# A transformer block on eight cores: mean subtraction moved from Pool to VectorE, squares to ScalarE, last norm's sums ahead of a projection

## The chip, the cores and the metric

The kernel runs on one Trainium2 chip, on 8 cores, each with one of the eight sequences of the batch; the cores exchange nothing. The time is that of the slowest core, in microseconds (us). On a core, TensorE (PE in the rows) multiplies matrices, VectorE (DVE), ScalarE (ACT) and GpSimd (Pool) work element by element, and SyncE (SP) issues the DMAs.

## The reference

```python
def reference(x, Q_w, ..., O_w, O_b, U1, V1, b1, U2, V2, b2):   # x: (8, 2048, 1024) f32
    x = x + 0.5 * ffn(layernorm(x))
    x = x + attention(layernorm(x))      # 16 heads of 64, causal, softmax
    x = x + 0.5 * ffn(layernorm(x))
    return x
def ffn(x):                              # rank 256, 4096 hidden units
    return (gelu((x @ U1) @ V1 + b1) @ U2) @ V2 + b2
def layernorm(x):
    return (x - mean(x)) / sqrt(var(x) + 1e-5)
```

## The kernel before, in words

A core keeps its whole x (2048 tokens by 1024 features, f32) on chip, transposed: 8 tiles of 128 features on the partitions, the tokens in 4 chunks of 512 columns (`x[:, c, m, :]`). Its program has three parts.

The first FFN is `stream(F1, 4)`: 4 chunks of 32 steps. A step has two matmuls with V1 (`ffn_v1`, L253, L255), one GELU on ScalarE (L260), and two matmuls with U2 for the step two before (`ffn_u2`, L270). Everything else is hung into these steps by `put(chunk, step, function, ...)`, so each engine's queue gets it in that order. For chunk c that is, one chunk ahead, casts and squares of x (`ln1_prep`) and their sums over the features by matmuls with ones (`ln1_stat`), and at step 23 (29 in chunk 0) the reciprocal root and U1 (`f1_break`). For the chunk before, it is the eight output tiles (`ln2_tile`: two matmuls with V2 and, on VectorE, the addition to x, L295), the squares of each pair of tiles (`ln_square`), their sums (`ln2_stat`) and the scaling to bf16 (`ln2_scale`, L519). The half product of a chunk is evicted to `qm` at step 1 of the next (L279, L281). V2 and b2 are centred over the features at the end of chunk 0 (`center_v2`), so the FFN's output has mean zero once the mean of x is taken out of x (`x_center`, L484, one call a tile); what is taken out, with the mean of the FFN's output (`mean_out`), goes to DRAM and is added back to x in the second FFN (`mean_in`, L1449). So the second norm needs only the mean of squares.

Attention is a list of 320 steps, 40 for each of 8 head pairs (rounds). A step is two score matmuls (`qk_step`, L1033), one exponential on ScalarE (L1046), for the last blocks of a row a mask on Pool (L1055), and three steps later two matmuls with V (`av_step`, L1071). Between the steps, filler is drawn from a generator: in each round the projections of the next (`qk_proj`, `v_proj`), row maxima (`norm`, L735), and the bound that the exponential subtracts (`bound`, `bound_root`, `bound_out`). `share` says how many units of 216 ns of filler stand drawn after each step. A clock kept by the planner, `now`, advances by these estimates; `soon(ns, fn)` puts a piece of work off by that much of `now`, and `run_due` issues what is due. The two filler PSUM banks, 6 and 7, take turns (`main_bank`, `side_bank`).

Round 0 begins with the `bridge`: the last values of the first half, the output tiles of chunk 3 with its squares on ScalarE, its mean, the query and key projections of chunk 2, the sums, the root (`root`, L973 and L975) and the eight scalings of chunk 3, alternately on VectorE and Pool, two pairs of value projections with two row maxima among them, and the query and key projections of chunk 3, which read the scaled chunk 3. The zeros of the query buffer of round 1 are written by Pool as soon as the first FFN is over (`q_zeros(0)`, L890).

The second FFN is again a stream of 4 chunks. In it the mean is loaded at step 0 of a chunk and added at steps 20 to 27 on Pool; the next chunk's casts are on VectorE and its squares on Pool at steps 8 to 14; a chunk's outputs leave in the next chunk.

An engine works its queue in order. `Q.need(...)` is a wait on semaphores that Q's queue makes before its next instruction.

## Time and profile before

| | |
|---|---|
| median of 3 runs | 896.29 us |
| lowest and highest run | 896.21 and 990.42 us |
| profiled execution, whole | 894.62 us |
| its span, slowest core | 893.1 us (all cores 887.8 to 893.1) |
| TensorE busy | 825.9 us |
| VectorE, ScalarE, Pool busy | 418.8, 626.7, 280.2 us |
| mean granted TensorE clock | 0.985 of full |

One execution is profiled and the slowest core shown; starts count from the beginning of its span. The highest run stands far from the other two, which differ by 0.1 us. A wait in the rows is the idle time of an engine before an instruction, with the instruction that ended it.

### The profile page before, as it was taken

The page shows a single profiled execution, that of the slowest core. Times are in us where ns is not written, and L with a number is a line of the kernel's source. Part 1 is how long each engine was busy: PE and PEld are TensorE (multiplying, and loading weights), DVE is VectorE, ACT ScalarE, POOL GpSimd, SP SyncE. Part 2 cuts the span into 40 slices and gives each one's busy share as a digit, 9 for nine tenths or more (in the row PEclk, how much of TensorE's full clock was granted, in tenths as well). Part 3 has the DMA queues.
Part 4 walks back from the last instruction along what each step waited for, and adds up shares of the span by engine and source line. Part 5 has one row for each costly group of instructions (what it writes and reads, how often), then busy time and mean ns, then how long its engine had stood idle before and what let it go on. Part 6 is the DMA issues. An engine that isn't in the chain of part 4 may idle for free.

```text
span 893.1 us, 13052 instructions; the slowest of 8 cores (887.8 to 893.1 us)
## 1 busy us (share of the span) xinstructions
PE 825.9 (92%) x4122; PEld 398.3 (45%) x4122; DVE 418.8 (47%) x635; ACT 626.7 (70%) x791; POOL 280.2 (31%) x269
## 2 busy tenths in 40 slices
PE   4899889998699899999999999999789999999997
PEld 1344334543345445455454554544344444444442
DVE  2366666645556473643737436366243341233122
ACT  2665555557466688888888988899765636766764
POOL 0554975212423121312213122121232134071910
PEclk9899999999899999999999999999999999999999
DMA  9899001000012000300003000023600011022122
GB/s 261 257 334 313 18 25 48 1 1 1 1 58 97 1 1 1 107 24 25 1 1 107 25 25 1 1 78 112 212 0 1 1 31 18 31 77 84 24 94 95
DMA packets 17929, 57.83 MB, mean 65 GB/s; under 512 B 2116, under 2 KB 3524, under 8 KB 17352
## 3 DMA queue, kind: packets, MB, share of 16 engines
q1 hardware_dynamic: 17864, 57.00, 20.7%
q8 instruction: 36, 0.59, 0.3%
q14 instruction: 29, 0.24, 0.1%
HBM read 43.35 MB, written 13.64 MB: 64 GB/s over the span
## 4 chain that ended last, share of the span: by engine, by line
PE 77%; DVE 9%; issue 6%; ACT 5%; DMA 1%; POOL 1%; DVEq 0%; SPq 0%; ACTq 0%; POOLq 0%
PE ps L1033 12%; PE ps L270 12%; PE ps L1071 10%; PE ps L674 9%; PE ps L823 6%; PE ps L1228 6%; PE ps L253 6%; PE ps L255 6%; PE ps L194 3%; ACT pt L1046 2%; PE ps L226 2%; DVE QZ L697 2%; PE ps L731 2%; DVE yb L519 1%; PE ps L288 1%
## 5 line engine op out<-in xcount | busy, mean ns | idle before, releaser
L1046 ACT ACTIVATE pt<-ps,small 128x1024 bf16<-128x1024 f32 x320 | 321.2, 1026 | 98.6 <-PE ps L1033 91.7
L260 ACT ACTIVATE hb<-ps,cols 128x512 bf16<-128x512 f32 x256 | 173.5, 688 | 105.0 <-PE ps L255 104.2
L1055 POOL TENSOR_TENSOR pt<-pt,cb 128x256 bf16<-128x256 bf16 x128 | 85.8, 681 | 347.8 <-ACT pt L1046 300.7
L1033 PE MATMUL ps<-QZ,KM 128*128 128x512 bf16 (+1 forms) x640 | 177.6, 359 | 7.0 <-ACT pt L1046 5.8
L1071 PE MATMUL ps<-pt,V 128*128 128x512 bf16 (+3 forms) x640 | 170.8, 349 | 0.2 <-POOL pt L1055 0.2
L674 PE MATMUL ps<-yb,wqk 128*128 128x512 bf16 x512 | 139.8, 380 | 2.2 <-DVE small L735 1.1
L1071 PEld LDWEIGHTS ps<-pt,V 128*128 128x128 bf16 x640 | 62.6, 98 | 66.7 <-issue 2.9
L1033 PEld LDWEIGHTS ps<-QZ,KM 128*128 128x128 bf16 x640 | 60.6, 99 | 70.3 <-issue 25.6
L823 PE MATMUL ps<-wvb,yb 128*128 128x256 bf16 x512 | 74.1, 277 | 7.3 <-DVE small L735 6.6
L270 PE MATMUL ps<-hb,u2b 128*128 128x512 bf16 x256 | 78.1, 391 | 2.2 <-ACT hb L260 2.1
L270 PE MATMUL ps<-hb,u2c 128*128 128x512 bf16 x256 | 75.3, 379 | 1.8 <-ACT hb L260 1.4
L1096 DVE TENSOR_TENSOR attn<-ps,LR 64x512 bf16<-64x512 f32 x64 | 44.0, 688 | 59.0 <-ACT LR L1092 58.4
L674 PEld LDWEIGHTS ps<-yb,wqk 128*128 128x128 bf16 x512 | 48.5, 98 | 50.2 <-issue 5.7
L295 DVE SCALAR_TENSOR_TENSOR x<-ps,small,x 128x512 f32<-128x512 f32 x64 | 47.2, 749 | 44.5 <-PE ps L290 43.6
L697 DVE TENSOR_SCALAR QZ<-ps,cols 64x512 bf16<-64x512 f32 x64 | 47.9, 748 | 34.8 <-PE ps L674 27.1
L823 PEld LDWEIGHTS ps<-wvb,yb 128*128 128x128 bf16 x512 | 49.8, 99 | 31.2 <-issue 9.5
L1228 PE MATMUL ps<-attn,wo 128*128 128x512 bf16 x256 | 61.9, 379 | 1.4 <-DVE x L1238 0.8
L735 DVE TENSOR_REDUCE small<-ps 128x1 f32<-128x512 f32 x64 | 44.1, 689 | 28.3 <-PE ps L731 26.3
L253 PE MATMUL ps<-pb,v1b 128*128 128x512 bf16 x128 | 50.6, 395 | 3.3 <-DVE pb L236 3.3
L255 PE MATMUL ps<-pb,v1b 128*128 128x512 bf16 x128 | 50.3, 393 | 0.0
L484 POOL TENSOR_TENSOR x<-x,mu 128x512 f32<-128x512 f32 x32 | 45.8, 1461 | 12.6 <-DVE mu L450 12.6
L253 PE MATMUL ps<-pb,v1c 128*128 128x512 bf16 x128 | 48.5, 379 | 0.1
(133 smaller groups left out, 919.4 us busy)
## 6 DMA issues: line engine op xcount, KB each, us to landing
x<-x SPq DMA_DIRECT2D x16, 512.0 KB, 12.6
out<-x SPq DMA_DIRECT2D x32, 256.0 KB, 2.1
stg<-u SPq DMA_DIRECT2D x10, 512.0 KB, 11.5
stg<-v SPq DMA_DIRECT2D x10, 512.0 KB, 10.7
wos<-wo SPq DMA_DIRECT2D x8, 512.0 KB, 4.2
wst<-wq SPq DMA_DIRECT2D x7, 512.0 KB, 3.9
wst<-wk SPq DMA_DIRECT2D x7, 512.0 KB, 4.3
wst<-wv SPq DMA_DIRECT2D x6, 512.0 KB, 8.0
```

What stands on the lines that cost most here:

```text
L253: PE.run(lambda e: e.matmul(ps[:, b, :], F["v1"][:, fc // 4, 0, 128 * (fc % 4):128 * (fc % 4 + 1)], F["pb"][:, c % 2, 0, :], start=True, s ...
L255: t = PE.do(lambda e: e.matmul(ps[:, b, :], F["v1"][:, fc // 4, 1, 128 * (fc % 4):128 * (fc % 4 + 1)], F["pb"][:, c % 2, 1, :], start=Fals ...
L260: F["t_gelu"][g] = ACT.do(lambda e: e.activation(F["hb"][:, g % 4, :], ps[:, b, :], AF.Gelu_apprx_tanh, bias=cols[:, C_B1 + fc:C_B1 + fc + ...
L270: f = lambda e, m=m: e.matmul(ps[:, 3 + m, :], F["u2"][:, fc, 128 * m:128 * (m + 1)], F["hb"][:, g % 4, :], start=(fc == 0), stop=(fc == N ...
L674: f = lambda e, k=k: e.matmul(ps[:, b, :], wqk[:, which, k, :], yb[:, ch, k, :], start=(k == 0), stop=(k == NM - 1))
L697: toks.append(DVE.do(lambda e, r=r, h=h: e.tensor_scalar(QZ[s][r, h, csl], ps[r, b, :], cols[r, C_QB + p:C_QB + p + 1], None, OP.add)))
L823: f = lambda e, k=k, kt=kt, o=o: e.matmul(ps[:, b, o:o + 256], yb[:, kt // 4, k, 128 * (kt % 4):128 * (kt % 4 + 1)], wvb[:, k, :], start=( ...
L1033: f = lambda e, j=j, kt=kt: e.matmul(ps[:, 2 * sl + j, lo:TC], KM[s][:, 128 * kt:128 * (kt + 1)], QZ[s][:, h, TC * c + lo:TC * (c + 1)], s ...
L1046: t_e[i] = ACT.do(lambda e: e.activation(pt[:, i % 4, :, lo:TC], ps[:, 2 * sl:2 * sl + 2, lo:TC], AF.Exp, bias=bias, scale=0.125))
L1055: L["pt", i] = POOL.do(lambda e, v=v: e.tensor_tensor(v, v, mask, OP.mult))
L1071: f = lambda e, kt=kt, lo=lo, j=j: e.matmul(ps[:, b, lo:TC], V[gr % 2][:, kt, pr, 64 * h:64 * h + 128], pt[:, i % 4, j, lo:TC], start=(kt ...
L1228: f = lambda e, k=k: e.matmul(ps[:, b, :], wo[:, m, k, :], attn[:, c, k, :], start=(k == 0), stop=(k == NP - 1))
```

## The change

Seven things change. The subtraction of the mean (`x_center`) goes to VectorE and, for chunks 1 to 3, to steps 0, 1, 2, 5, 8, 11, 20 and 21 of the chunk itself, where it stood one chunk ahead. The squares of the second norm go to ScalarE for all chunks, at once after their tile for the first three. In the bridge the sums of chunk 3 come before the key projection of chunk 2, the root 400 ns of `now` after them, and all eight scalings are on VectorE, put off by 1500 + 700 m; filler issues them all before the query projection of chunk 3. The first score matmuls of round 0 wait for the zeros of their own buffer alone (`t_z[:2]`). The share of filler in round 0 begins at 13 units and grows by 4 for four steps, then by 6.5; in rounds 0 to 5 it ends one step later. The root of a round's bound is asked for 2700 after its last maximum, then each 1200, where it was 2300 and 900. In the second FFN the mean is added on VectorE at steps 22 to 29.

```diff
--- before.py
+++ after.py
@@ -480,8 +480,8 @@
 
     def x_center(c, m):
 
-        POOL.need(t_mu[c], L["c", c][m // 2])
-        F1["t_xin"][c, m] = POOL.do(lambda e: e.tensor_tensor(
+        DVE.need(t_mu[c], L["c", c][m // 2])
+        F1["t_xin"][c, m] = DVE.do(lambda e: e.tensor_tensor(
             x[:, c, m, :], x[:, c, m, :], mu[c], OP.subtract))
 
     def mean_out(c, b):
@@ -501,8 +501,7 @@
         t = ffn_v2(F1, c, m, b)
         if m % 2:
             def square():
-                q = ACT if c == NCH - 1 else POOL
-                L.setdefault(("s2", c), []).append(ln_square(q, m // 2, x[:, c], t, L["sqf"], sq))
+                L.setdefault(("s2", c), []).append(ln_square(ACT, m // 2, x[:, c], t, L["sqf"], sq))
             if c == NCH - 1:
                 soon(1500, square)
             else:
@@ -561,9 +560,8 @@
     put(0, 31, center_v2)
     for m in range(NM):
         put(0, 4 + 3 * m, x_center, 0, m)
-        put(1, 14 + m, x_center, 1, m)
-        put(1, 24 + m, x_center, 2, m)
-        put(2, 22 + m, x_center, 3, m)
+        for c in range(1, NCH):
+            put(c, (0, 1, 2, 5, 8, 11, 20, 21)[m], x_center, c, m)
     for c in range(1, NCH):
         for m in range(8):
             put(c, 3 + (3 * m) // 2, ln2_tile, c - 1, m, (7, 5, 6)[m % 3])
@@ -962,7 +960,6 @@
         yield 1
         yield 1
         yield from qk_proj(0, 0, 2)
-        yield from qk_proj(0, 1, 2, ACT)
         if len(L["s2", 3]) < 4:
             run_due(1e12)
         b = main_bank()
@@ -974,15 +971,18 @@
             ACT.need(tl)
             L["r2", 3] = ACT.do(lambda e: e.activation(rstd[:, 0, :], var[:, 0, :], AF.Exp, scale=-0.5))
             for m in range(NM):
-                ln2_scale(3, m, POOL if m % 2 else DVE, 0)
+                soon(1500 + 700 * m, lambda m=m: ln2_scale(3, m, DVE, 0))
 
         for m in range(NM):
             yield 1
-        root()
+        soon(400, root)
+        yield from qk_proj(0, 1, 2, ACT)
         yield from norm_mid(0, v_proj(0, 8), [(0, 2)])
         yield from norm_mid(0, v_proj(0, 10), [(1, 2)])
         bound0((2,))
         soon(1500, lambda: bound0_root((2,)))
+        while t_yb[3] is None:
+            run_due(agenda[0][0])
         yield from qk_proj(0, 0, 3)
         wqk_cast(1, 0)
         if ("u0", 2) not in L:
@@ -1023,7 +1023,7 @@
         lo = 256 if r == n - 1 else 0
         sl = i % 2
         if p == 0:
-            PE.need(t_z, t_QK[0, 0, c], [t_QK[0, 1, j] for j in range(c + 1)])
+            PE.need(t_z[:2], t_QK[0, 0, c], [t_QK[0, 1, j] for j in range(c + 1)])
         PE.need(t_e.get(i - 2), t_QK[p] if p else None)
         if i < 2:
             PE.need(bank_free[2 * sl], bank_free[2 * sl + 1])
@@ -1153,7 +1153,7 @@
             bank_at = now[0] + 1300
             if n == 7:
                 bound(p + 1)
-                root_at = now[0] + 2300
+                root_at = now[0] + 2700
 
         def small(n, u):
             nonlocal root_at
@@ -1161,7 +1161,7 @@
                 yield from one_norm(pend.pop(0))
             elif root_at is not None and ("u", p + 1) not in L and now[0] >= root_at:
                 bound_root(p + 1)
-                root_at += 900
+                root_at += 1200
             elif root_at is not None and ("u", p + 1) in L and now[0] >= max(root_at, bank_at) and u <= 5:
                 root_at = None
                 yield from bound_out(p + 1)
@@ -1384,10 +1384,10 @@
                 win = window(p) if p < NP - 1 else window7()
                 acc = 0
                 if p == 0:
-                    share = {k: 6.0 * (k + 1) for k in range(12)}
-                    share.update({k: 72 + v for k, v in spread(p, 12, 37, 24 + 96 + 9).items()})
+                    share = {k: 13 + 4 * k if k < 4 else 25 + 6.5 * (k - 3) for k in range(12)}
+                    share.update({k: 77 + v for k, v in spread(p, 12, 38, 19 + 96 + 9).items()})
                 elif p < NP - 2:
-                    share = spread(p, 0, 37, 96 + 9)
+                    share = spread(p, 0, 38, 96 + 9)
                 elif p == NP - 2:
                     share = spread(p, 0, 35, 64 + 9)
                 else:
@@ -1445,8 +1445,8 @@
         t_mu2[c] = ld_mu2[c % 2].load(SP, mu2[:, c % 2, :], s_mu[c:c + 1, :].partition_broadcast(128))
 
     def mean_in(c, m):
-        POOL.need(t_mu2[c], L["c3", c][m // 2], t_x2[c][m])
-        F2["t_xin"][c, m] = POOL.do(lambda e: e.tensor_tensor(
+        DVE.need(t_mu2[c], L["c3", c][m // 2], t_x2[c][m])
+        F2["t_xin"][c, m] = DVE.do(lambda e: e.tensor_tensor(
             x[:, c, m, :], x[:, c, m, :], mu2[:, c % 2, :], OP.add))
 
     def out_tile(c, m, b):
@@ -1479,7 +1479,7 @@
             put(c, 21, f2_break, c)
         put(c, 0, mean_load, c)
         for m in range(8):
-            put(c, 20 + m, mean_in, c, m)
+            put(c, 22 + m, mean_in, c, m)
     stream(F2, NCH)
     for m in range(NM):
         out_tile(3, m, (5, 6, 7)[m % 3])
```

## Rows read from the trace of the kernel before

**Rows 1.** Page, busy time, share and instructions of TensorE and its weight loads.

```profile
PE 825.9 (92%) x4122; PEld 398.3 (45%) x4122; DVE 418.8 (47%) x635; ACT 626.7 (70%) x791; POOL 280.2 (31%) x269
```

**Rows 2.** Table of stretches: length, busy time by engine, PEclk, DMA share, GB/s.

```profile
205.00:262.00 57.00, 44.36 (x238) 23.33 (x236) 28.57 (x45) 34.30 (x46) 20.98 (x19) 0.94 0.02 3
...
303.00:359.00 56.00, 54.02 (x302) 28.95 (x303) 28.98 (x49) 48.61 (x59) 11.22 (x16) 1.00 0.00 1
```

**Rows 3.** TensorE's waits, 60 to 125 us: total, times, longest.

```profile
PE ps L288 <- DVE qm L279: 4.7, 2, 2.9
PE ps L194 <- DVE yb L178: 2.7, 1, 2.7
```

**Rows 4.** TensorE's waits, 205 to 250 us.

```profile
PE ps L823 <- DVE small L735: 5.9, 1, 5.9
PE ps L731 <- ACT var L973: 1.6, 1, 1.6
PE ps L288 <- DVE x L295: 1.3, 2, 0.6
PE ps L1033 <- ACT pt L1046: 1.0, 1, 1.0
PE ps L674 <- DVE small L806: 0.9, 1, 0.9
PE ps L1033 <- POOL QZ L890: 0.7, 1, 0.7
```

**Rows 5.** Timeline, chunk 1: start, duration, instruction, idle time before it.

```profile
87.39 12.97 POOL L484 TENSOR_TENSOR x<-x,mu 128x512 f32<-128x512 f32 x8
...
91.25 1.75 DVE L178 CAST yb<-x 128x1024 bf16<-128x1024 f32 x1
...
108.78 10.39 DVE L519 TENSOR_TENSOR yb<-x,rstd 128x512 bf16<-128x512 f32 x8
```

**Rows 6.** Timeline, the end of chunk 0.

```profile
70.54 0.68 DVE L279 TENSOR_SCALAR qm<-ps 128x512 bf16<-128x512 f32 x1
...
71.47 0.38 PE L288 MATMUL ps<-qm,v2b 128*128 128x512 bf16 x1 [1.77 <-DVE qm L279]
```

**Rows 7.** Timeline, the last scalings and a row maximum.

```profile
231.70 5.70 DVE L519 TENSOR_TENSOR yb<-x,rstd 128x512 bf16<-128x512 f32 x4 [4.88 <-ACT rstd L975]
...
237.92 0.67 DVE L735 TENSOR_REDUCE small<-ps 128x1 f32<-128x512 f32 x1
```

**Rows 8.** Groups by line: min/median/max ns (or, last two, busy, mean, idle).

```profile
L484 POOL TENSOR_TENSOR x<-x,mu x32: 1262/1284/1777, 24.8 to 156.2; 128x512 f32<-128x512 f32 x32
...
L186 POOL TENSOR_TENSOR sq<-x x12: 1893/1894/2342, 74.9 to 181.6; 128x1024 bf16<-128x1024 f32 x12
...
L519 DVE TENSOR_TENSOR yb<-x,rstd x8: 681/686/693, 198.7 to 203.8; 128x512 bf16<-128x512 f32 x8
...
L185 ACT ACTIVATE sq<-x x4: 1042/1044/1047, 214.8 to 221.8; 128x1024 bf16<-128x1024 f32 x4
...
L260 ACT ACTIVATE hb<-ps,cols 128x512 bf16<-128x512 f32 x256 | 173.5, 688 | 105.0 <-PE ps L255 104.2
...
L295 DVE SCALAR_TENSOR_TENSOR x<-ps,small,x 128x512 f32<-128x512 f32 x64 | 47.2, 749 | 44.5 <-PE ps L290 43.6
```

**Rows 9.** Table of stretches around waits.

```profile
95.00:100.00 5.00, 3.51 (x11) 1.43 (x12) 2.91 (x3) 0.60 (x1) 5.00 (x4) 0.75 0.01 3
...
120.00:125.00 5.00, 4.97 (x24) 2.29 (x25) 1.82 (x3) 2.06 (x3) 1.52 (x1) 1.00 0.00 2
235.00:240.00 5.00, 1.26 (x7) 0.92 (x8) 4.19 (x5) 0.00 (x0) 4.15 (x4) 0.74 0.00 0
240.00:245.00 5.00, 5.00 (x21) 2.81 (x20) 1.76 (x5) 1.56 (x4) 0.67 (x1) 0.57 0.00 0
```

**Rows 10.** Timeline, the end of chunk 2.

```profile
167.91 0.38 PE L288 MATMUL ps<-qm,v2b 128*128 128x512 bf16 x1 [0.19 <-ACT qm L281]
```

**Rows 11.** TensorE's waits, 360 to 600 us.

```profile
PE ps L761 <- ACT small L755: 2.2, 4, 0.5
```

## The prediction

> **What bounds the kernel now.** I read the shares of the page first [rows 1]: TensorE is busy 825.9 us, 92% of the span. So only its idle time, some 67 us, and time at a lower clock can be won, and the table of stretches says where it lies. The attention rounds lose little: 303 to 359 is 56.00 us with 54.02 busy, clock 1.00. The stretch 205 to 262, in which the last FFN tiles of chunk 3, its second norm and the first attention steps share the engines, is 57.00 us with 44.36 busy and clock 0.94 [rows 2]: 12.6 us idle and 0.06 x 57 = 3.4 us of clock. Then the table of TensorE's waits of each such stretch: who ended them. Between 60 and 125 us it names two [rows 3]; between 205 and 250 five that matter [rows 4]. Last the timeline around the longest, to see what the releasing engine had been doing [rows 5, 6, 7].
>
> **Work leaves Pool.** The mean's subtraction costs Pool 1.28 us (median) each, 32 times, and the squares 1.89 each, 12 times [rows 8]. Neither is on TensorE's path itself; the harm is what VectorE does meanwhile. Eight scalings ran at 10.39 / 8 = 1.30 us apart beside a busy Pool, and a cast took 1.75 [rows 5]; the same scaling takes 0.686 with Pool idle [rows 8], some 0.62 apart in a row of them. That the neighbour is the cause is a reading: nothing else differs so plainly. The Trainium skill's page SBUF — State Buffer, section "SBUF: two separate sides", says that a VectorE instruction with two SBUF inputs and a Pool instruction that reads SBUF lock each other out for a whole instruction. By that rule the scalings fall to the lone pace once Pool is quiet; if instead the slow pace had another cause it would stay, and chunk 1 would keep its waits (the third rival). The trace agrees with the rule, 1.30 against 0.62.
>
> **Chunk 1 of the first FFN, the sums of the next chunk.** TensorE waits 2.7 us for a cast [rows 3], and in 95 to 100 the clock is 0.75 [rows 9]: 0.25 x 5 = 1.3 us. Pool had eight subtractions in a row from 87.39 to 100.4 [rows 5]. After the change none stands there. Four casts, four squares and two smaller evictions, ten pieces of about 0.69 each, are 6.9 us; TensorE's own work up to there (four steps of 0.86, the mean's matmuls, the eight of the sums) is some 7. Saved: 2.7 + 1.3 = 4.0 us; bounds 2.7 and 4.7.
>
> **Chunk 1, its end.** The eviction of the half product waits behind the eight slow scalings; of all such waits (4.7 us, two [rows 3]) this one is 2.9. Scalings at 0.62 end near 108.78 + 5.0 = 113.8, before the eviction can start at about 116.3. Two subtractions of chunk 2 now stand ahead of it, 1.24 us, ready earlier too. The same place one chunk later, with Pool's scalings out of the way, waits 0.19 [rows 10]. Saved 2.7; bounds 1.5 and 2.9.
>
> **Chunk 0, its end.** Here the eviction stands behind the centring of V2 and starts at 70.54, and TensorE waits 1.77 us for it [rows 6]. The subtractions of chunk 1 are now queued at steps 0 and 1, ahead of it: 2 x 0.62 = 1.2 us later, all of it on the path. The wait of 3.0 us could cost clock as well: after a wait of 2.9 us the next slice showed 1.00, after 5.9 us 0.57 [rows 9, 4]. So 1.2, bounds 0 and 3.0.
>
> **Squares on ScalarE.** The trace has four of them, 1.044 us each [rows 8]. Twelve more stand between the GELUs, four a chunk, one in three steps with two output tiles. Three steps are, for TensorE, 3 x 4 + 4 matmuls at 0.216 us (1.73 us for each of the eights) = 3.46 us; for ScalarE 3 x 0.69 + 1.05 = 3.12. It fits, barely. Each square also waits for VectorE's eviction, some 0.5 us after its GELU, so the next GELU comes about 1 us late, and TensorE runs its second product two steps behind: it feels 0 to 0.1 us. I take 0.5 us in all; bounds 0 and 6 (0.5 for each of 12). Subtractions at steps 5, 8 and 11 lie between pairs of tiles and cost VectorE only slack.
>
> **First attention steps.** The first score matmul waits 0.7 us for Pool to write zeros that another buffer needs [rows 4]; the narrower wait removes that. More filler ahead of the first steps (13 units, then 4 a step, against 6 a step) puts an output tile where TensorE waits 1.0 for an exponential, and spreads the rest, where it waits 1.3 for evictions [rows 4]. Stepping through the order with two matmuls of 0.216 a tile and an eviction of 0.75 [rows 8], the last tile ends near 215.5 with one step pair (0.86) less done, against 218.7: 2.4 us saved; bounds 0.7 and 3.
>
> **The last sums and scalings.** This is the largest term. From 231.70 four scalings on VectorE take 5.70 us, 1.42 each, with the other four on Pool beside them, and a row maximum of 0.67 us stands behind them; TensorE waits 5.9 for it, after 1.6 for the bank which the root's first half holds [rows 7, 4]. In 235 to 245 the clock is 0.74 and 0.57, with 1.26 and 5.00 busy [rows 9]: 0.26 x 1.3 + 0.43 x 5 = 2.5 us of clock (up to 3.4 by the whole stretch). Then 0.9 for the copy of the exponent's shift [rows 4]. Together 1.6 + 5.9 + 2.5 + 0.9 = 10.9 us. After the change the sums come before the key projection of chunk 2, whose 1.73 us then cover the root, and the scalings are queued 0.7 us apart, so a maximum has at most one or two before it. What becomes late next: the squares of chunk 3 on ScalarE, as the sums come some 5 us sooner (0.7 us), and the eight scalings, 5.0 us, with about 4.5 us of maxima and evictions between them must be done before the query projection of chunk 3. 18 units of filler and three steps, some 6.3 us of TensorE's work, lie between; 9.5 less 6.3 and less the 1.8 by which the first scaling can start ahead of that work leave a wait of 1.4 us. The shift's 0.9 stays. 10.9 - 0.7 - 1.4 - 0.9 = 7.9, saved; bounds 4 and 10.
>
> **Attention rounds.** The root of each round's bound is asked for 0.4 us later and the filler ends one step later. TensorE waits for that root 2.2 us in four rounds [rows 11]; some of it may go, or return where the filler runs out. I take 0.8 saved, bounds 3 saved and 2 lost. Second FFN: the mean is added by VectorE, 0.69 against Pool's 1.26, in steps 22 to 29, when VectorE has nothing to do and no output waits; 0. Cover gone (it would have to pass the next eviction): 0.7.
>
> **The sum.** 4.0 + 2.7 - 1.2 - 0.5 + 2.4 + 7.9 + 0.8 = 16.1 us. The profiled execution took 894.6 us (span 893.1 and 1.5 around it), so 878.5; the median of the runs shown is 896.3, 1.7 more. I put the time at 880.2 against that median, -1.8%. Two per cent, about what a measurement of this kernel can tell from no change, is 17.9 us: the boundary is 878.4.
>
> **Rivals.**
> First: *the scalings are cleared wholly* (the window 225 to 250 falls to the pace of the later rounds, no new wait). For it: a later round loses 2 us in 56 [rows 2]. Then 10 instead of 7.9, 3 instead of 2.4, 2 instead of 0.8 in the rounds, and nothing for the squares: 4.0 + 2.7 - 1.2 + 3 + 10 + 2 = 20.5, so 875.8 against the median. Chance 0.33.
> Second: *the stall moves inside the bridge*. All scalings now lie on one engine, which also evicts values and takes maxima; if they bunch because the root is late, a maximum again has several before it, TensorE idles some 3 to 4 us and the clock falls once more. For it: TensorE's whole 5.9 us wait came from one maximum behind queued scalings. Against it: 0.62 each instead of 1.42. Then 7.9 becomes 2, the total 10.2: 886.1. Chance 0.14.
> Third: *VectorE's slow pace is not Pool's doing*. Then casts and scalings stay slow, chunk 1 keeps its 4.0 and 2.7, and the added operations bunch the bridge by 3: 894.6 - 16.1 + 6.7 + 3 = 888.2, 889.9 against the median. Chance 0.04.
> Fourth, slower than before: *the squares hold up the GELUs*. A square waits for an eviction with the GELUs behind it. TensorE's page (TensorE: Matmul & The Clock Gate, "Architectural detail: the array is 16× 32×32") says that ScalarE's queue is strictly in order, so nothing passes a waiting square. As a mechanism of this kernel: if GELUs have less lead than I count, each of the 12 squares costs TensorE 0.5 of waiting and 1.05 of work, 18.6 us, more than the 16.1 + 0.5 won: 894.6 + 2.0 + 1.7 = 898.3. It decides from 16.6 / 12 = 1.4 us a square. Against it: ScalarE is idle 105.0 us over 256 GELUs [rows 8], 0.41 a step, and 1.73 us of extra matmuls go with each two squares. Chance 0.03.
>
> **How the numbers follow.** The forecast 0.46, the rivals 0.33, 0.14, 0.04, 0.03. The likeliest is 880.2. The forecast's own terms range from about 875 to 885. The range 872.5 to 888.0 takes in the first and second rival and leaves out the last two and the extremes of the first. Faster by over 2% is the first rival (0.33, of which a little falls short) and a part of the forecast's lower side, 0.38 in all; within 2% 0.60; slower by over 2% 0.02, as the fourth alone would have to cost twice its price.
>
> **What would show it.** Scalings and casts at about 0.69 in chunk 1, no wait of the sums near 93 us and no slice below 1.00 there; a wait near 3 us at the end of chunk 0; squares of 1.05 between GELUs without TensorE waiting for them; the first score matmul not waiting for Pool; no wait above 2 us and no slice at half clock between 215 and 250. I am wrong if VectorE stays at 1.3 us with Pool idle, or if a new wait above 3 us stands before the query projection of chunk 3.

## The result and the profile after

The changed kernel takes 874.73 us (median of 4 runs: 874.05, 874.41, 875.05 and one of 896.72), the kernel before 896.21 and 896.29 beside it: ratio 0.9757, of the medians without the 896.72, with a 95% interval of [0.9729, 0.9786]. Executions in which one die ran at a lower clock for long stand in no comparison, here and below. On another chip a kernel whose instruction lists are the changed kernel's on every engine (a2 below) took 874.83 against 894.57, ratio 0.9782 [0.9766, 0.9797]; this one has the narrower footing and is used below. So the change wins 19.5 us, -2.2%. The forecast was 880.2 in a range of 872.5 to 888.0: the time is in the range and 5.5 us below the forecast, nearest to the first rival's 875.8.

The page, busy time by engine, to be read against [rows 1]:

```profile
PE 819.7 (94%) x4122; PEld 397.2 (45%) x4122; DVE 448.3 (51%) x703; ACT 638.0 (73%) x803; POOL 166.1 (19%) x189
```

Pool lost 114 us of work and VectorE gained 29.5, ScalarE 11.3. TensorE's busy time fell by 6.2 us with the same 4122 matmuls, which speaks of the clock. Its idle time fell from 893.1 - 825.9 = 67.2 to 873.5 - 819.7 = 53.8.

Where the 19.6 us between the two spans (893.1 and 873.5) were won is read from landmarks: matmuls and evictions that both kernels have once. First the kernel before, then the changed one, in the timeline: the first and the last small matmul of the bridge, the one at the end of round 0, the one ahead of the last round, and the last half product.

```profile
209.53 0.58 PE L800 MATMUL ps<-small,cfs 128*128 128x2 f32 x4 [0.50 <-DVE V L836]
262.17 0.58 PE L800 MATMUL ps<-small,cfs 128*128 128x1 f32 x4 [0.64 <-ACT small L793]
303.83 0.58 PE L761 MATMUL ps<-small,cfs 128*128 128x1 f32 x4 [2.81 <-ACT small L755]
632.65 0.58 PE L761 MATMUL ps<-small,cfs 128*128 128x1 f32 x4 [2.42 <-ACT small L755]
882.34 0.69 DVE L279 TENSOR_SCALAR qm<-ps 128x512 bf16<-128x512 f32 x1 [17.97 <-PE ps L270]
```

```profile
203.59 0.58 PE L798 MATMUL ps<-small,cfs 128*128 128x2 f32 x4 [0.50 <-DVE V L834]
246.64 0.50 PE L798 MATMUL ps<-small,cfs 128*128 128x1 f32 x4
287.22 0.58 PE L759 MATMUL ps<-small,cfs 128*128 128x1 f32 x4 [0.95 <-DVE V L834]
612.10 0.99 PE L759 MATMUL ps<-small,cfs 128*128 128x1 f32 x4 [2.43 <-ACT small L753]
862.79 0.69 DVE L279 TENSOR_SCALAR qm<-ps 128x512 bf16<-128x512 f32 x1 [13.16 <-PE ps L270]
```

The lead of the changed kernel is 5.9 us at the first pair, 15.5 at the second, 16.6, 20.6 and 19.6 at the others. So the first FFN gave 5.9, the bridge 9.6, the rest of round 0 1.1, rounds 1 to 6 together 3.9, and the last round with the second FFN took 1.0 back.

The slowest core is another one in each kernel (4 before, 7 after), and not all of the 5.9 is the change's. ScalarE evicts its part of the half product of chunk 0 at 69.09 before and at 67.57 after; over the eight cores that time spreads from 63.8 to 69.1 before and from 64.4 to 67.6 after, and as widely in kernels whose instructions up to there are the same. So 1.5 of the 5.9 is where these two cores happened to stand. The medians over the eight cores of each profiled execution, in us:

| stretch | before | after |
|---|---|---|
| start to that eviction in chunk 0 | 66.8 | 66.2 |
| to the first small matmul of the bridge | 142.2 | 136.0 |
| to the last of the bridge | 52.7 | 43.0 |
| to the one at the end of round 0 | 41.7 | 40.6 |
| rounds 1 to 6 | 328.8 | 324.7 |
| last round, to the first half product of the second FFN | 141.3 | 142.2 |
| to the last half product | 108.4 | 108.4 |
| to the end | 9.9 | 10.9 |

"By landmarks" below means these stretches.

**First FFN.** TensorE's waits between 60 and 125 us, of the changed kernel, against [rows 3]:

```profile
PE ps L288 <- DVE qm L279: 3.0, 1, 3.0
```

The cast and the second `qm` are gone, and one wait of 3.0 us stands where 1.8 stood. Its timeline at the end of chunk 0, and below it the stretches around it and around the chunk 1 sums:

```profile
69.03 1.29 DVE L484 TENSOR_TENSOR x<-x,mu 128x512 f32<-128x512 f32 x2
70.23 0.69 DVE L279 TENSOR_SCALAR qm<-ps 128x512 bf16<-128x512 f32 x1
71.17 0.38 PE L288 MATMUL ps<-qm,v2b 128*128 128x512 bf16 x1 [2.99 <-DVE qm L279]
73.22 0.63 PE L253 MATMUL ps<-pb,v1b 128*128 128x512 bf16 x1
```

```profile
70.00:75.00 5.00, 3.83 (x11) 1.45 (x12) 2.27 (x4) 0.62 (x1) 0.00 (x0) 0.67 1.05 360
95.00:100.00 5.00, 5.00 (x25) 2.25 (x23) 2.95 (x4) 2.10 (x4) 1.94 (x2) 1.00 0.39 133
```

The two subtractions stand ahead of the eviction, as the forecast said, and TensorE waits 1.2 us more. After the wait a matmul takes 0.63 instead of 0.38 and the clock of the slice is 0.67: another 0.33 x 5 = 1.65 us. On one of the eight cores, core 3, the same wait cost no clock (last section). At the sums of chunk 1 (95 to 100) the 0.75 of [rows 9] has become 1.00.

**Bridge.** The stretch that [rows 2] shows with 44.36 busy at 0.94:

```profile
205.00:262.00 57.00, 51.36 (x282) 26.71 (x281) 36.97 (x64) 40.76 (x51) 14.63 (x17) 1.00 0.14 41
```

TensorE's waits, 195 to 250 us, against [rows 4]:

```profile
PE ps L1071 <- POOL V L882: 1.8, 1, 1.8
PE ps L729 <- DVE V L834: 1.4, 1, 1.4
...
PE ps L672 <- DVE yb L518: 0.7, 1, 0.7
```

The waits for the maximum (5.9), for the root's bank (1.6), for an exponential (1.0) and for Pool's zeros (0.7) are gone. Two are new: 1.8 for Pool's writing of ones into V (it begins at 242.58, behind a mask, and takes 1.81; before, at 258.4, nobody waited for it), and 1.4 for an eviction of values that stands behind paced scalings. What the paced scalings look like, in the timeline of VectorE and TensorE:

```profile
221.29 0.69 DVE L733 TENSOR_REDUCE small<-ps 128x1 f32<-128x512 f32 x1
221.90 0.68 DVE L518 TENSOR_TENSOR yb<-x,rstd 128x512 bf16<-128x512 f32 x1
...
227.04 0.59 PE L672 MATMUL ps<-yb,wqk 128*128 128x512 bf16 x2 [0.67 <-DVE yb L518]
```

A maximum goes through between scalings, and the query projection of chunk 3 waits 0.67 us.

### The profile page after: what moved, and what is told of

It is laid out like the page before. It is cut to its first block, busy times and chain, and to the rows that moved or that the text cites. A ratio compares the mean times of both kernels' runs of the same rounds, so it can differ in the third digit from the quotient of the medians.

```text
span 873.5 us, 13011 instructions; the slowest of 8 cores (870.0 to 873.5 us)
## 1 busy us (share of the span) xinstructions
PE 819.7 (94%) x4122; PEld 397.2 (45%) x4122; DVE 448.3 (51%) x703; ACT 638.0 (73%) x803; POOL 166.1 (19%) x189
## 4 chain that ended last, share of the span: by engine, by line
PE 79%; ACT 6%; DVE 6%; issue 5%; DMA 2%; POOL 0%; DVEq 0%; SPq 0%; ACTq 0%; POOLq 0%
PE ps L1033 12%; PE ps L672 12%; PE ps L270 11%; PE ps L1071 11%; PE ps L1228 6%; PE ps L253 6%; PE ps L255 6%; PE ps L821 4%; PE ps L194 4%; ACT pt L1046 3%; PE ps L226 2%; PE ps L288 1%; PE ps L290 1%; DMA stg<-v 1%; PE ps L729 1%
## 5 line engine op out<-in xcount | busy, mean ns | idle before, releaser
L1033 PEld LDWEIGHTS ps<-QZ,KM 128*128 128x128 bf16 x640 | 60.7, 99 | 67.6 <-issue 22.5
L270 PE MATMUL ps<-hb,u2b 128*128 128x512 bf16 x256 | 76.2, 383 | 2.6 <-ACT hb L260 2.1
L253 PE MATMUL ps<-pb,v1c 128*128 128x512 bf16 x128 | 48.5, 379 | 0.1
L255 PE MATMUL ps<-pb,v1c 128*128 128x512 bf16 x128 | 48.5, 379 | 0.0
```

The lines of the kernel that those rows point to most:

```text
L253: PE.run(lambda e: e.matmul(ps[:, b, :], F["v1"][:, fc // 4, 0, 128 * (fc % 4):128 * (fc % 4 + 1)], F["pb"][:, c % 2, 0, :], start=True, s ...
L255: t = PE.do(lambda e: e.matmul(ps[:, b, :], F["v1"][:, fc // 4, 1, 128 * (fc % 4):128 * (fc % 4 + 1)], F["pb"][:, c % 2, 1, :], start=Fals ...
L270: f = lambda e, m=m: e.matmul(ps[:, 3 + m, :], F["u2"][:, fc, 128 * m:128 * (m + 1)], F["hb"][:, g % 4, :], start=(fc == 0), stop=(fc == N ...
L1033: f = lambda e, j=j, kt=kt: e.matmul(ps[:, 2 * sl + j, lo:TC], KM[s][:, 128 * kt:128 * (kt + 1)], QZ[s][:, h, TC * c + lo:TC * (c + 1)], s ...
```

## The experiments

My theory, once the result was known: the gain has four sources (VectorE rid of Pool's company in the first FFN, the bridge's order, its pacing, and something in the rounds that I had priced too low), each to be found again by undoing it alone. The rival: the gain is the bridge's, and the rounds drift with whatever state the bridge leaves them in. All kernels are the changed one with the edit shown, except e1. The kernel before took 894.46, 894.57, 894.89 and 896.03 us on the four chips, so a part's worth is told from the ratio: (ratio - 0.9782) x 895. Each ratio is uncertain by some 1.5 us, a difference of two by some 2; where that is too coarse, the landmarks of all eight cores are set beside it.

**The rounds: a1, a2, a3.** Both round edits undone, then each alone:

```diff
-                root_at = now[0] + 2700
+                root_at = now[0] + 2300              # a1, a2
-                root_at += 1200
+                root_at += 900                       # a1, a2
-                    share = spread(p, 0, 38, 96 + 9)
+                    share = spread(p, 0, 37, 96 + 9)   # a1, a3
```

> The changed kernel with the root of each round's bound asked for at 2300 and 900 again, and the filler of rounds 1 to 5 ending at step 37 again. The changed kernel's rounds 1 to 6 are 3.9 us shorter than before (54.9 against 55.5 us a round). If these two edits did that, this kernel takes 874.7 + 3.9 = 878.6 us and its rounds are 55.5 us long. If the forecast's 0.8 us was right and the rounds are shorter for another reason (what they inherit from round 0), it takes about 875.5 us and its rounds stay at 54.9.

> The changed kernel with only the times of the bound's root as before (2300 and 900). Undoing both edits of the rounds cost 3.7 us (878.4). Theory: the later root gives it, since asked for early it sits in ScalarE's queue ahead of the exponential and TensorE waits 0.5 us for it, then for the exponential, at the narrow last step of a row: 877 to 878.4, rounds of 55.3 to 55.5 us. Rival: the filler's one step more (37 to 38) gives it, and this kernel stays at 874.7 to 875.5 with rounds of 54.9.

> The changed kernel with only the filler of rounds 1 to 5 ending one step earlier again (37). Theory that the root gives the gain: 874.7 to 875.5. Rival: the filler's extra step gives it: 877 to 878.4 and rounds of 55.3 to 55.5 us, with TensorE idle at the end of a round.

Measured: a1 878.37, ratio 0.9817 [0.9802, 0.9832]; a2 874.83, 0.9782 [0.9766, 0.9797]; a3 875.41, 0.9781 [0.9766, 0.9797]. Together the edits are worth 3.1 us, each alone nothing by the ratio: a2's instruction lists are even those of the changed kernel, so the later root alone moves nothing once the filler ends a step later. By landmarks rounds 1 to 6 take 328.5 us in a1, 324.7 in a2 and 326.0 in a3, so a3 has lost 1.2 of the 3.8 there, and its total hides it (its last round is 0.6 shorter). One round, from one root to the next, in a1 and then in the changed kernel (table of stretches):

```profile
386.84:442.27 55.43, 54.29 (x300) 28.59 (x301) 28.77 (x48) 49.53 (x59) 12.61 (x19) 1.00 0.03 11
```

```profile
392.07:447.08 55.01, 54.03 (x300) 28.61 (x301) 29.84 (x48) 49.70 (x59) 12.42 (x18) 1.00 0.00 1
```

0.42 us in this round; the three others between such roots differ by 0.9 each (a1 222.3 us for the four, the changed kernel 219.2), 3.1 in all. Where it comes from, in the timeline of a1 around the bound's root (L751 and L753; the small matmuls behind it are L759):

```profile
441.82 0.20 ACT L753 ACTIVATE small<-small 128x1 f32<-128x1 f32 x1
441.93 0.67 ACT L1046 ACTIVATE pt<-ps,small 128x512 bf16<-128x512 f32 x1
442.27 0.58 PE L759 MATMUL ps<-small,cfs 128*128 128x1 f32 x4 [0.55 <-ACT small L753]
...
443.40 2.20 ACT L1046 ACTIVATE pt<-ps,small 128x1024 bf16<-128x1024 f32 x2 [0.80 <-PE ps L1033]
```

and of a2, the same place:

```profile
446.15 0.20 ACT L753 ACTIVATE small<-small 128x1 f32<-128x1 f32 x1
446.38 1.12 ACT L1046 ACTIVATE pt<-ps,small 128x1024 bf16<-128x1024 f32 x1
446.61 0.58 PE L759 MATMUL ps<-small,cfs 128*128 128x1 f32 x4 [0.35 <-ACT small L753]
...
448.17 1.12 ACT L1046 ACTIVATE pt<-ps,small 128x1024 bf16<-128x1024 f32 x1 [0.16 <-PE ps L1033]
```

In a1, as before, the root falls into the narrow last step of a row: its exponential has 512 columns and lasts 0.67, not 1.12. TensorE stands 0.55 us in front of the small matmuls, the next scores come late, and ScalarE, with so short an exponential to bridge it, idles 0.80. In a2 the root falls into a full step: 0.35, then 0.16. The waits from 330 to 600 us, TensorE's and then ScalarE's, of a1:

```profile
PE ps L759 <- ACT small L753: 3.0, 5, 0.8
```

```profile
ACT pt L1046 <- PE ps L1033: 24.0, 56, 0.8
```

and of the changed kernel:

```profile
PE ps L759 <- ACT small L753: 1.8, 5, 0.4
```

```profile
ACT pt L1046 <- PE ps L1033: 20.8, 60, 0.8
```

TensorE's own wait is 1.2 us longer in a1, ScalarE's for scores 3.2 us, which is the size of the whole loss.

The other rounds show the same: behind the root ScalarE's exponential lasts 0.67 five times in a1 and five times before, and 1.10 or 1.12 each time in a2, a3 and the changed kernel. Either edit takes the root out of the narrow step, which is why neither alone is missed much. The rival falls here: a1 has the bridge of the changed kernel (43.0), and its rounds have the pace of before (55.53 before, from 405.11 to 460.64).

**The mean and the squares in the first FFN: b1, b2, b3, b3r.** b1 gives the subtraction back to Pool at its old steps (which is not its old time, see below), b2 to Pool at the new steps, b3 and b3r the squares of chunks 0 to 2 back to Pool.

```diff
-        DVE.need(t_mu[c], L["c", c][m // 2])
-        F1["t_xin"][c, m] = DVE.do(lambda e: e.tensor_tensor(
+        POOL.need(t_mu[c], L["c", c][m // 2])                      # b1, b2
+        F1["t_xin"][c, m] = POOL.do(lambda e: e.tensor_tensor(     # b1, b2
-        for c in range(1, NCH):
-            put(c, (0, 1, 2, 5, 8, 11, 20, 21)[m], x_center, c, m)
+        put(1, 14 + m, x_center, 1, m)                             # b1
+        put(1, 24 + m, x_center, 2, m)                             # b1
+        put(2, 22 + m, x_center, 3, m)                             # b1
-                ... ln_square(ACT, m // 2, x[:, c], t, L["sqf"], sq)
+                ... ln_square(ACT if c == NCH - 1 else POOL, ...)  # b3, b3r
```

> The changed kernel with the subtraction of the mean on Pool again, at the steps of before. Theory: Pool beside VectorE slows the casts and scalings of chunk 1; the waits of 2.7 us for the cast and 2.9 us for the half product come back and the one at the end of chunk 0 falls from 3.0 to 1.8 with its clock loss: 4.0 + 2.7 - 1.2 to 2.8, so 4 to 5.5 us more, 879 to 880. Rival: the squares, now on ScalarE, were the harmful part of Pool's load, and with them gone Pool's subtractions cost nothing: 873 to 875.

> The changed kernel with the subtractions on Pool, but at the changed steps (chunks 1 to 3: 0, 1, 2, 5, 8, 11, 20, 21). It parts the engine from the place. If the harm of before is Pool's instructions beside VectorE's casts and scalings, the new place alone takes most of them away from these: 875 to 876.5, and the wait at the end of chunk 0 falls below 3.0 since VectorE no longer has the two subtractions ahead of the half product's eviction (unless these wait for Pool's lock on the centring of V2). If the engine matters wherever it stands: 879 to 880 as with both undone.

> The changed kernel with the squares of chunks 0 to 2 on Pool again. Theory: they cost TensorE nothing on ScalarE (0.5 us at most) and little on Pool, where only the casts of the next chunk meet them: within 1 us of 874.7, and VectorE's casts near them take 1.0 to 1.9 instead of 0.69. Rival: Pool's squares delay the sums of each chunk, 2 us or more.

> The changed kernel with the squares of chunks 0 to 2 on Pool again, once more. The one undisturbed look gave 877.3, with a wait of 1.0 us for the cast ahead of the sums in chunk 1. Theory: Pool's squares push into VectorE's casts there, as before: 876 to 877.5. Rival: the squares are worth nothing and the look was high: 874.5 to 875.5.

Measured: b1 879.52, 0.9829 [0.9812, 0.9845], so 4.2 us; b2 876.33, 0.9784 [0.9763, 0.9805]. b3 gave a single time to go by, 877.32 beside 894.46, and no ratio, so it was repeated as b3r: 876.22, 0.9784 [0.9767, 0.9801]. So of b1's 4.2 us most is the place. The engine alone and the squares lie within the error: 0.2 each by the ratio, though b2 stands 1.5 us above a2 on the same chip, and b3's time 2.4 above 0.9782 of the 894.46 beside it. By landmarks the first FFN takes 136.0 in the changed kernel, 139.8 in b1, 136.6 in b2, 137.2 in b3 and 136.8 in b3r: 3.8, 0.6, 1.2 and 0.8 more; the last three are small beside the 1.7 by which cores of one kernel differ there. TensorE's waits 60 to 125 us of b1, then of b3r (b2 has one wait for `qm`, 3.7):

```profile
PE ps L288 <- DVE qm L279: 7.1, 2, 3.7
```

```profile
PE ps L288 <- DVE qm L279: 3.0, 1, 3.0
PE ps L194 <- DVE yb L178: 1.2, 1, 1.2
```

b1 has two `qm` waits again but not the cast's, and the one at the end of chunk 0 is 3.7, not the 1.8 that I expected back; the squares alone bring back 1.2 of the cast's 2.7. Pool's timeline in b1 shows why:

```profile
59.23 10.29 POOL L484 TENSOR_TENSOR x<-x,mu 128x512 f32<-128x512 f32 x8 [0.74 <-DVE mu L450]
```

Pool works its queue in order. In the kernel before, the four squares of chunk 0 stood ahead of chunk 1's subtractions and held them back to 87.39 [rows 5], onto the casts. With the squares on ScalarE the same eight, at the same steps, start at 59.23, as soon as the mean is there, and fall onto the centring of V2; in b2 they do too, at 59.74. So b1 does not undo the subtraction as it was: the cast's 2.7 needed Pool's squares ahead of Pool's subtractions, and no run has these subtractions back at their old time with the squares on ScalarE. What b1 and b2 differ in is chunk 2's subtractions, eight in a row from 98.6 to 109.4 in b1, with Pool's casts of weights behind them. What it costs VectorE to have Pool beside it shows in b1's scalings of chunk 1:

```profile
105.38 10.92 DVE L518 TENSOR_TENSOR yb<-x,rstd 128x512 bf16<-128x512 f32 x8
```

They take 4.90 in the changed kernel. In b2 (and b1) the same is true of the centring of V2 ahead of `qm`: its cast L375 lasts 1.28 beside Pool's subtraction and 0.22 without, which makes 3.0 us of waiting 3.7.

**The bridge whole: b4.** Key projection ahead of the sums, root at once, scalings at once and alternately on Pool, the old share and the wait for all zeros:

```diff
+        yield from qk_proj(0, 1, 2, ACT)       # ahead of the sums
-        soon(400, root)
+        root()
-                soon(1500 + 700 * m, lambda m=m: ln2_scale(3, m, DVE, 0))
+                ln2_scale(3, m, POOL if m % 2 else DVE, 0)
-                    share = {k: 13 + 4 * k if k < 4 else 25 + 6.5 * (k - 3) for k in range(12)}
+                    share = {k: 6.0 * (k + 1) for k in range(12)}
-            PE.need(t_z[:2], ...)
+            PE.need(t_z, ...)
...  (and without the loop that issues all scalings ahead of the query projection)
```

> The changed kernel with the bridge as before: sums after the key projection, root at once, scalings alternating between VectorE and Pool and all at once, the old share of round 0, the wait for all zeros. Theory: the bridge is worth 9.8 to 10.5 us by itself, so 884.5 to 885.2, with the wait of some 6 us and slices at half clock back. Rival: the first FFN's part hands the bridge a better start, and the bridge alone is worth 6 or less: 881 or less.

Measured: 885.17, 0.9897 [0.9881, 0.9914], so the bridge is worth 10.3 us (by landmarks 8.8 in it and 1.1 in the rest of round 0). Its waits are those of before, and so is the clock behind them (waits 195 to 250 us, and a stretch):

```profile
PE ps L821 <- DVE small L733: 5.9, 1, 5.9
PE ps L729 <- ACT var L971: 1.6, 1, 1.6
```

```profile
235.00:240.00 5.00, 5.00 (x23) 2.82 (x21) 1.76 (x5) 1.72 (x4) 0.67 (x1) 0.65 0.00 0
```

**Inside the bridge: c1, c2, c3, and e1 on the kernel before.** c1 keeps the pacing but has the scalings alternately on VectorE and Pool. c2 has all on VectorE but asks for them at once. c3 puts the key projection ahead of the sums again and keeps the rest. e1 is the kernel before with that one order changed.

```diff
-                soon(1500 + 700 * m, lambda m=m: ln2_scale(3, m, DVE, 0))
+                soon(1500 + 700 * m, lambda m=m: ln2_scale(3, m, POOL if m % 2 else DVE, 0))   # c1
+                ln2_scale(3, m, DVE, 0)        # c2
```

```diff
-        yield from qk_proj(0, 1, 2, ACT)       # e1: ahead of the sums, in the kernel before
...
         root()
+        yield from qk_proj(0, 1, 2, ACT)       # e1: behind the root; c3 is the reverse
```

> The changed kernel with the last eight scalings again alternately on VectorE and Pool, but still paced 700 apart. The bridge is worth 10.4 us in all. Theory: Pool's share makes VectorE's scalings slow (1.4 instead of 0.7 us) and Pool's own take 1.7, so the chunk is ready later and the maxima wait: 2 to 4 us more, 877 to 879. Rival: pacing alone takes care of it, as two engines share the work: 874 to 875.5.

> The changed kernel with all eight scalings on VectorE but queued at once after the root. Theory: a maximum or an eviction stands behind up to eight scalings of 0.62 us, 5 us; the sums' early place leaves some 2 us of cover, so a wait of 2 to 3 us and perhaps clock: 876.5 to 879. Rival: they start earlier than paced ones and are cleared before the first maximum is due, so the time is 873.5 to 875.

> The changed kernel with the key projection of chunk 2 again ahead of the sums, so only the order undone; scalings stay on VectorE and paced. Theory: without these 1.7 us of cover TensorE waits for the bank that the root holds (1.6 us as before) and for the scaled chunk (1 to 2 us more): 877 to 878.5. Rival: engine and pacing alone give the gain, 874.7 to 875.5.

> The kernel before with one edit: the key projection of chunk 2 after the sums and the root. Scalings still alternate, unpaced. If the order carries the bridge, its 1.7 us of filler and a step hide the 1.6 us wait for the bank and part of the 5.9 us wait, and with them the half clock: 5 to 8 us less than before, 887 to 890. If the maximum behind four slow scalings (5.7 us) still stops TensorE, it gains 1.5 to 3 us: 892 to 893.

Measured: c1 874.38, 0.977 [0.9755, 0.9785]; c2 877.89, 0.9805 [0.9788, 0.9821]; c3 883.84, 0.9867 [0.9846, 0.9889]; e1 891.9, 0.996 [0.9945, 0.9976]. So the engine of the scalings is worth nothing that can be told (-1.1; by landmarks c1's bridge is 0.5 longer and its rounds 0.6 shorter), which misses my theory of 2 to 4. The pacing is worth 2.1: the intervals overlap in part, but c2's bridge is 2.2 to 2.4 longer on every core. The order is worth 7.6 taken out last (6.1 to 8.2 by landmarks) and 0.004 x 895 = 3.6 put in first. Waits 195 to 250 us of c2, then of c3, then of e1 (200 to 255, lines of before):

```profile
PE ps L821 <- DVE small L733: 3.0, 1, 3.0
```

```profile
PE ps L672 <- DVE yb L518: 4.7, 1, 4.7
PE ps L729 <- ACT var L971: 2.4, 1, 2.4
```

```profile
PE ps L823 <- DVE small L735: 3.5, 1, 3.5
```

c2 has the second rival's mechanism: a maximum stands behind eight scalings in a row (5.38 us in its timeline), yet it costs 3.0 us, since they take 0.67 each. c3 shows what the order hides: with the sums late, paced scalings are too late for the query projection. Pacing pays only with the sums early; e1 shows that early sums take 2.4 of the 5.9 us off even with all scalings at once and half of them on Pool.

**Mean in the second FFN back on Pool: a4.**

```diff
-        DVE.need(t_mu2[c], L["c3", c][m // 2], t_x2[c][m])
-        F2["t_xin"][c, m] = DVE.do(lambda e: e.tensor_tensor(
+        POOL.need(t_mu2[c], L["c3", c][m // 2], t_x2[c][m])
+        F2["t_xin"][c, m] = POOL.do(lambda e: e.tensor_tensor(
-            put(c, 22 + m, mean_in, c, m)
+            put(c, 20 + m, mean_in, c, m)
```

> The changed kernel with the mean added back on Pool again, at steps 20 to 27 of the second FFN. The forecast's term is 0: nothing waits for it and VectorE has no fast SBUF work beside it; 874.7 within 0.5. Rival: Pool's additions slow something of the second FFN, 1 us or more.

Measured: 873.56, 0.976 [0.9743, 0.9778]. That is 2.0 us less than the changed kernel, with intervals that just touch; its times (873.05 to 873.80) lie below all eight of a2 and a3 on the same chip (874.60 to 876.98). TensorE's waits from 640 to 880 us are the same four lines in both, and from 720 to 800 its busy time is 78.87 in both. So VectorE for this addition brings nothing, and the landmarks say what it costs: from the last half product to the end a4 takes 9.7 to 10.3 us on its eight cores, the kernel before 9.7 to 10.8 and the changed kernel 10.6 to 11.9; medians 9.8, 9.9 and 10.9. The last computing instruction ends 7.1 us after that eviction in all of them; why the outputs then end later is not shown. What else a4 is ahead by is not the edit's: up to the second FFN its instructions are the changed kernel's, and four of its cores, against one of the changed kernel's, happened to lose no clock at the end of chunk 0.

**Repairs of what the change left: d1, d2, d4.** d1 lets the values' product wait for the ones of its own buffer only. d2 centres the first half of V2 two steps earlier and apart from the second. d4 has both, and the first two subtractions behind the eviction of `qm`.

```diff
-        PE.need(L["pt", i], [...], t_one)
+        PE.need(L["pt", i], [...], t_one[gr % 2])       # d1, d4
-    put(0, 31, center_v2)
+    put(0, 29, center_v2, (0,))                         # d2, d4, ahead of f1_break
+    put(0, 31, center_v2, (1,))
-            put(c, (0, 1, 2, 5, 8, 11, 20, 21)[m], x_center, c, m)
+            put(c, (2, 2, 5, 5, 8, 11, 20, 21)[m], x_center, c, m)   # d4
```

> The changed kernel with the value matmuls waiting only for the ones of their own buffer. Its trace shows one wait of 1.8 us for the other buffer's. Theory: all of it is on the path: 872.9. Rival: the mask of that step, behind the ones on Pool, takes its place: 874 to 874.7.

> The changed kernel with half of V2's centring moved into VectorE's idle time ahead of the first break; subtractions stay ahead of the eviction. It takes 2.4 us from the eviction's queue: the wait of 3.0 us falls to 0.6 and the slice at 0.67 to 1.00: 2.4 + 1.6 = 4.0 less, 870.7. Rival: the half in front delays the break itself by as much: 873 to 874.7.

> The changed kernel with three repairs for waits that its trace shows: half of the centring of V2 in VectorE's idle time ahead of the first break and the first two subtractions of a chunk behind the half product's eviction (wait of 3.0 us at the end of chunk 0, with a slice at 0.67), and the value matmuls waiting only for the ones of their own buffer (1.8 us). Theory: 3.0 + 1.6 of clock + 1.8 = 6.4 less what remains for the tiles, so 869 to 870. Rival: what is gained at the end of chunk 0 is lost to tiles waiting for evictions behind the subtractions, and the ones only move the wait to the mask: 872.5 or more.

Measured: d1 871.44, 0.9735 [0.9718, 0.9752]; d2 870.48, 0.9724 [0.9707, 0.9741]; d4 868.07, 0.9697 [0.9683, 0.9711]. So 4.2, 5.2 and 7.6 us below the changed kernel; d4 is the fastest of all, 3.0% below the kernel before. In d1 the wait for `V` L882 is gone. In d4 there is no wait for VectorE's `qm` at the end of chunk 0, and the clock there stays up:

```profile
70.00:75.00 5.00, 5.00 (x25) 2.25 (x23) 3.98 (x6) 3.80 (x6) 0.00 (x0) 1.00 1.07 339
```

d2 leaves 0.5 of the 3.0 us wait; 2.5 and the 1.65 of clock are 4.15 of its 5.2, and by landmarks its first FFN is 4.15 shorter (131.85 on all eight cores). d1's bridge is 1.9 shorter on every core; another 1.0 lies in the last round, where on six of its cores the clock fell less than in the changed kernel though the instruction lists are the same, so that microsecond is not the edit's; the rest of its 4.2 is within the error. By the ratios the two gains don't add up in d4 (4.2 and 5.2 against 7.6), by landmarks they do: 131.7 in the first FFN and 41.1 in the bridge. Only on two cores, the slowest among them, the query projection's wait for the exponent's shift (`small` L804, L805 in d4's numbering) is 1.5 against 0.7 and the bridge 42.8. d4's later subtractions add 0.2 us to what d2 has.

## Where the prediction held and where it failed, point by point

The direction, the place of the largest term and its size were right; the forecast fell short by 3.4 us of 19.5 (16.1 forecast). I had called a gain within 2%, that is a time above 878.4, the likelier outcome (0.60 against 0.38), and that was wrong: the gain is 2.2%.

- **The step that failed: "Attention rounds. ... I take 0.8 saved, bounds 3 saved and 2 lost."** Measured 3.9 over rounds 1 to 6 (landmarks), 3.1 by a1, so 3.1 or 2.3 of the shortfall of 3.4, and by either beyond my bound of 3. The place that I named, TensorE's wait for the root [rows 11], was right, and the size was off: that wait fell by 1.2 us over five roots, but ScalarE's idle time behind it by 3.2. I read TensorE's own waits alone, in rounds in which TensorE and ScalarE both have little slack (54.29 and 49.53 busy of 55.43 us in a1); the exponential after the root, narrow or full, should have been looked at.
- **First FFN: 5.0 forecast (4.0 + 2.7 - 1.2 - 0.5), 5.9 measured.** Chunk 1's cast wait and its clock went, as forecast; before, 100 to 105 stood at 0.91 too, 0.45 us that I had not counted. The second `qm` wait went whole, 2.9 against 2.7. The end of chunk 0 cost 1.2 as forecast plus 1.65 of clock, 2.85 and near the bound of 3.0; I chose the lower value because a wait of 2.9 us [rows 3] was followed by 1.00 [rows 9], and that comparison did not hold: it was one core's, and on six of the eight cores of that same execution the wait at that place, 3.0 to 3.5 us, was followed by 0.66 to 0.70. These come to 4.0 + 0.45 + 2.9 - 2.85 = 4.5, and from the eviction in chunk 0 on the two cores differ by 140.4 - 136.0 = 4.4; the other 1.5 of the 5.9 is the start. So on these two cores the 5.0 was a little high. Over the medians the stretch gave 6.2, since most cores of before lost clock a second time.
- **Squares on ScalarE: 0.5 lost by the forecast, 0.2 (b3r) to 2.4 (b3's one time) won, 0.8 and 1.2 by landmarks.** TensorE's waits for GELUs, 60 to 125 us, are 1.0 in two with and without them. The fourth rival is refuted: twelve squares of 1.06 us each found their room. The sign was off because I gave the squares no part in the cast's delay, of which b3r shows 1.2 us, and did not see that they held Pool's subtractions back onto the casts.
- **First steps, sums and scalings: 10.3 forecast (2.4 + 7.9), 9.6 measured in the bridge and 10.3 by b4.** The size was right, the parts less so: the query projection waits 0.7 instead of 1.4, and the wait for the values (1.4) and for the ones (1.8) I had not seen. Against them, the clock gave more than the 2.5 that I took, 0.94 to 1.00 over 57 us, 3.4, and 1.3 of waiting for evictions of chunk 3 became 0.4.
- **Second FFN: 0 forecast.** No wait of TensorE's changed, but the end came 1.0 us later (medians), which a4 gives back. On the two slowest cores it does not show (10.8 and 10.7).
- **Last round: not in the sum.** 1.0 us lost. The wait ahead of it is the same (2.42 and 2.43 us), its price is not, see below.
- **Rivals.** The first gave the right time by partly wrong terms: the bridge was not cleared wholly, the rounds gave 3.9 and not 2. The second is c2's world, 3.0 us of waiting, which pacing avoids. The third is refuted: scalings beside a silent Pool take 4.90 for eight, and 10.92 again in b1.

## What to carry to other kernels

Where two engines are both nearly full, a small piece on the path is priced by what each of them does next: put it into a wide step, not into the narrow last one, and read both engines' waits. Pace work that someone waits for at the end, but only after its input has been made early: undoing the order alone cost 7.6 us, the pacing alone 2.1. And when an operation moves, look for what it now stands in front of: the two subtractions ahead of an eviction cost 2.85 us, and moving half of what stood in front of them forward, into idle time, won 4.15 by landmarks. In an in-order queue what is taken away counts as well: with its squares gone, Pool ran the same subtractions 28 us earlier, onto other work of VectorE.

## What the runs showed of the hardware

**VectorE beside Pool.** It is not every VectorE instruction that Pool slows. The changed kernel, timeline:

```profile
90.06 1.38 POOL L903 CAST wqk<-stg 128x1024 bf16<-128x1024 f32 x1 [31.19 <-DMA stg<-wq]
90.64 1.33 DVE L186 TENSOR_TENSOR sq<-yb 128x1024 bf16<-128x1024 bf16 x1
91.90 0.68 DVE L514 COPY var<-ps 128x512 f32<-128x512 f32 x1
```

and the kernel before, VectorE while Pool has the row of eight subtractions of [rows 5]:

```profile
93.11 1.57 DVE L186 TENSOR_TENSOR sq<-yb 128x1024 bf16<-128x1024 bf16 x1
94.59 0.68 DVE L515 COPY var<-ps 128x512 f32<-128x512 f32 x1
95.19 1.15 DVE L178 CAST yb<-x 128x1024 bf16<-128x1024 f32 x1
```

The copy out of PSUM keeps its 0.68 beside Pool (second fence; in the first it runs between two of Pool's casts); the squares and the cast, which live in SBUF alone, do not. In the first fence the squares started 0.58 us into Pool's cast and ended 0.53 after it, where alone they take 0.69: they stood until Pool was nearly done. The Trainium skill, page SBUF — State Buffer, section "SBUF: two separate sides", has the lock for a whole instruction, taken by a VectorE instruction with two SBUF inputs or in a two-port mode. The squares, which read SBUF twice, agree with it; that the cast runs in such a mode no row shows, only that it is held up as the rule says for one that does.

**The same wait, another clock.** The 2.4 us wait ahead of the last round: the five us from 630 stand at a granted clock of 0.84 and the next at 0.82 before; from 610, at 0.60 and 0.72 after. That is 0.34 x 5 = 1.7 us of clock before and 0.68 x 5 = 3.4 after, for the same work with a different phase; it more than accounts for the 1.0 us taken back. The cores of one execution say it more plainly. At the end of chunk 0 all eight cores of the changed kernel wait 2.98 or 2.99 us, behind the same instructions. The five us from the wait's end, on core 7 and on core 3:

```profile
71.17:76.17 5.00, 5.00 (x16) 1.97 (x17) 2.02 (x4) 0.77 (x2) 0.00 (x0) 0.66 1.04 319
70.03:75.03 5.00, 5.00 (x24) 2.29 (x25) 2.86 (x5) 2.42 (x4) 0.00 (x0) 1.00 1.07 311
```

Seven cores stand at 0.66 to 0.71, one at 1.00, and its first FFN takes 134.3 us where the others take 135.7 to 136.0. In the kernel before, the wait there was 1.77 or 1.78 us on every core, and all eight stood at 1.00. So the length of a wait alone does not tell its price in clock, and neither does the program; what decides between the two was not tried.
